# A three-pass graph network in fp32 halves: one stage's stores on another queue, uniform tail rows, a split first block and four empty steps

## The reference

```python
def _gc(x, adj, W, b):
    return adj @ (x @ W) + b
h = jnp.maximum(_layernorm(x, axis=-1), 0.0)
h = relu(_gc(h, adj, W1, b1))
h = relu(_gc(h, adj, W2, b2))
out = x + _gc(h, adj, W3, b3)
```

## Time and profile before

| | |
|---|---|
| median of 3 runs | 1595.33 us (1593.61 to 1596.07) |
| profiled execution | 1592.36 us, span of its instructions 1590.6 us |
| PE busy | 1580.9 us (99%) |
| PEld, DVE, ACT, POOL busy | 86%, 55%, 38%, 29% |
| DMA | 303 MB, mean 191 GB/s |

### The profile page before, as it was taken

One profiled execution on the slowest core, in us unless ns is written; L12 is line 12 of the kernel. 1 busy time (PEld: TensorE's weight loads), 2 busy tenths in 40 slices (PEclk: granted clock), 3 DMA queues, 4 the chain that ended last, 5 costly groups with the idle time before them and its releaser, 6 DMA issues.

```text
span 1590.6 us, 20924 instructions
## 1 busy us (share of the span) xinstructions
PE 1580.9 (99%) x7674; PEld 1360.6 (86%) x7674; DVE 874.1 (55%) x1358; ACT 608.8 (38%) x1073; POOL 464.4 (29%) x417
## 2 busy tenths in 40 slices
PE   9999999999999999999999999999999999999999
PEld 7888889988889898989898989788898887888898
DVE  8973433256544443434564446664565537766856
ACT  5542222233433332323332333443455435454444
POOL 5864544336655000000000015345402314301302
PEclk9999999999999999999999999999999999999999
DMA  7966657744567554545455658883644437887866
GB/s 246 333 211 209 220 188 213 201 137 148 182 210 230 167 153 143 142 119 149 142 170 160 179 184 288 274 301 125 206 136 117 100 86 213 247 247 220 250 192 192
DMA packets 196628, 303.37 MB, mean 191 GB/s; under 512 B 22632, under 2 KB 92608, under 8 KB 196524
## 3 DMA queue, kind: packets, MB, share of 16 engines
q1 hardware_dynamic: 162268, 223.12, 47.4%
q0 software_dynamic: 12224, 43.16, 8.3%
q10 hardware_dynamic: 22032, 35.74, 6.3%
HBM read 219.44 MB, written 82.50 MB: 190 GB/s over the span
## 4 chain that ended last, share of the span: by engine, by line
PE 96%; DVE 1%; DMA 1%; POOL 1%; ACT 0%; issue 0%; SPq 0%; DVEq 0%; ACTq 0%
PE ps L1707 32%; PE ps L1708 32%; PE ps L1709 32%; PE ps L1795 1%; DVE ring L1336 1%; DMA raw<-TS 1%; POOL stash L1550 0%; PE ps L1740 0%; DMA xin<-x 0%; DVE parts L1479 0%; POOL stash L1552 0%; ACT ring L1119 0%; DVE S L1383 0%; POOL stash L1554 0%; DVE stats L1267 0%
## 5 line engine op out<-in xcount | busy, mean ns | idle before, releaser
L1336 DVE TENSOR_TENSOR ring<-raw,ring 128x512 fp32r<-128x512 f32 (+1 forms) x562 | 405.7, 734 | 424.7 <-ACT ring L1119 422.0
L1119 ACT CAST ring<-raw 128x512 fp32r<-128x512 f32 (+1 forms) x562 | 320.7, 577 | 560.2 <-PE ps L1709 465.2
L1707 PE MATMUL ps<-slots,still 128*128 128x512 f32 (+1 forms) x504 | 184.1, 365 | 1.8 <-DVE still L1308 1.7
L1708 PE MATMUL ps<-slots,still 128*128 128x512 f32 (+1 forms) x504 | 183.7, 365 | 0.0
L1709 PE MATMUL ps<-slots,still 128*128 128x512 f32 (+1 forms) x504 | 183.7, 364 | 0.0
L1708 PE MATMUL ps<-ring,even 128*128 128x512 f32 (+1 forms) x480 | 174.4, 363 | 0.0
L1707 PE MATMUL ps<-ring,even 128*128 128x512 f32 (+1 forms) x480 | 174.4, 363 | 0.0
L1709 PE MATMUL ps<-ring,even 128*128 128x512 f32 (+1 forms) x480 | 174.4, 363 | 0.0
L1563 POOL DMA_DIRECT2D prep<-P x40 | 26.5, 664 | 462.0 <-DMA P<-U 430.1
L1707 PE MATMUL ps<-ring,S 128*128 128x512 f32 (+1 forms) x420 | 153.4, 365 | 2.1 <-DVE ring L1336 1.9
L1708 PE MATMUL ps<-ring,S 128*128 128x512 f32 (+1 forms) x420 | 152.9, 364 | 0.0
(11 more groups left out here) (160 smaller groups left out, 2902.6 us busy)
## 6 DMA issues: line engine op xcount, KB each, us to landing
raw<-TS SPq DMA_DIRECT2D x160, 256.0 KB, 2.9
raw<-adjT SPq DMA_DIRECT2D x138, 256.0 KB, 3.2
raw<-adjT SPq DMA_DIRECT2D x41, 512.0 KB, 4.6
TS<-made SPq DMA_DIRECT2D x20, 1024.0 KB, 6.7
raw<-TS SPq DMA_DIRECT2D x80, 165.0 KB, 2.4
raw<-HS SPq DMA_DIRECT2D x50, 256.0 KB, 2.7
raw<-P SPq DMA_DIRECT2D x45, 256.0 KB, 3.9
raw<-adjT SPq DMA_DIRECT2D x68, 165.0 KB, 2.6
```

What stands on the lines that cost most here:

```text
L1119: act.copy(hi, src).then_inc(hi_done, 1)
L1336: dve.tensor_tensor(lo, src, hi.bitcast(F32), ALU.subtract).then_inc(lo_done, 1)
L1707: pe.matmul(out, st_hi, mv_hi, start=start, stop=False)
L1708: pe.matmul(out, st_hi, mv_lo, start=False, stop=False)
```

## The change

Four edits. (1) Four empty steps are put into `late` between the combines of pairs 8 and 9 and their S2 stationaries. (2) REP becomes 128, so that all operands of the short block have 128 rows or columns. (3) For the very first x block ACT and DVE work in four pieces of 128 columns, and PE waits for the piece that the column group m needs. (4) POOL issues the store of `made` itself, right behind the four operations of a pair; SP no longer does.

```diff
@@ w3_phase
                     for pair, bufs in ((8, a), (9, z)):
                         late.append(lambda pair=pair, bufs=bufs: combine(pair, bufs))
                         late.append(lambda: None)
+                    late.extend([lambda: None] * 4)
@@ gcn_kernel
-    REP = 2 * STEP + TAIL
+    REP = P
@@ sync
-            def store_made(i):
-                t = ORDER[i % PAIRS]
-                c = i // PAIRS
-                sp.wait_ge(made_done, 4 * (i + 1))
-                sp.dma_start(TS[t, :, :, within(c)], made[:, i % 2, :, 0:WIDTH[c]]).then_inc(made_stored[i % 2], 16)
...
-                while j.pair_freed is not None and stores < j.pair_freed:
-                    store_made(stores)
-                    stores += 1
...
-            while stores < made_total:
-                store_made(stores)
-                stores += 1
@@ scalar, cut1
+                    if n == 0:
+                        for m in range(KF):
+                            cols = slice(m * P, (m + 1) * P)
+                            act.activation(still[:, j.block, 0, cols], tile[:, cols], ACT.Relu,
+                                           scale=x_column(n, "scale")) \
+                                .then_inc(first_hi if m < KF - 1 else hi1_done, 1)
+                        root(1)
+                        centre(1)
+                        return
@@ vector, cut1
+                if j.kind == "x" and j.q == 0:
+                    for m in range(KF):
+                        cols = slice(m * P, (m + 1) * P)
+                        if m < KF - 1:
+                            dve.wait_ge(first_hi, m + 1)
+                        else:
+                            dve.wait_ge(hi1_done, j.cut + 1)
+                        dve.scalar_tensor_tensor(still[:, j.block, 1, cols], xin[:, j.block, 1, cols],
+                                                 x_column(0, "scale"),
+                                                 still[:, j.block, 0, cols].bitcast(F32), ALU.mult, ALU.subtract) \
+                            .then_inc(first_lo if m < KF - 1 else lo1_done, 1)
+                    return
@@ gpsimd, make
+                pool.wait_ge(made_done, 4 * (i + 1))
+                pool.dma_start(TS[ORDER[n], :, :, within(c)], made[:, i % 2, :, 0:w]) \
+                    .then_inc(made_stored[i % 2], 16)
@@ tensor, pass 1
-                    pe.wait_ge(lo1_done, j.ready)
+                    pe.wait_ge(lo1_done, j.cut + 1 if j.a == 0 else j.ready)
...
+                        if j.a == 0 and a == 0:
+                            if m < KF - 1:
+                                pe.wait_ge(first_lo, m + 1)
+                            else:
+                                pe.wait_ge(lo1_done, j.ready)
```

More of the change, by code:

```diff
@@ L769, in gcn_kernel @@
         lo1_done = sem("lo1_done")
+        first_hi = sem("first_hi")
+        first_lo = sem("first_lo")
         slot1_used = sem("slot1_used")
@@ L884, in load_x @@
                 sp.dma_start(xin[:, b, 1, :], x[b * P:(b + 1) * P, :]).then_inc(x_in[b], 16)
-            def store_made(i):
-                t = ORDER[i % PAIRS]
-                c = i // PAIRS
-                sp.wait_ge(made_done, 4 * (i + 1))
-                sp.dma_start(TS[t, :, :, within(c)], made[:, i % 2, :, 0:WIDTH[c]]).then_inc(made_stored[i % 2], 16)
-            stores = 0
             load_x(xs1[0])
```

## The result

The changed kernel is slower: median 1601.72 us of 11 runs (1595.37 to 1610.08), against 1593.61 us of 11 runs of the kernel before (1592.22 to 1598.83). The ratio is 1.0049, 95% interval 1.0035 to 1.0064, about 8 us. The forecast was 1592.0 us with a range up to 1595.8. The profiled execution took 1601.72 us (span 1599.9), so it stands at the median; that of before took 1592.36.

A forecast was written before the change was run, and what follows sets the result against it. PE, busy 1580.9 of 1590.6 us, was taken as the bound, with DVE near-bound from 20 to 68 us. The terms -1.4 - 2.1 + 0.4 - 0.2 = -3.3 us gave a median of 1592.0 us, range 1588.8 to 1595.8.

The forecast's parts named there:

- Edit 4: Stores of `made` issued by POOL: DVE about 0.5 us less busy before 68 us; -0.2 us, bounds -0.3 and +1.7.
- upper bound of 1.7 us: POOL back to back in pass 1's start, nearly one pair more before 68 us, costing 1.85 us of DVE.
- Rival C: In DVE's full stretch, POOL's descriptor writing keeps DVE's two-input operations out: +8 or so, net +5, 1600 us; chance 0.05.
- POOL's own numbers: For stores of `made` from POOL: issue about 1.1 us, landing 7 us, 7.7 us per pair, no holding by the store.
- Edit 1: Empty steps before the S2 to S4 stationaries remove PE's wait near 1326 us: -1.4 us, bounds -1.4 and -0.4.
- Rival D: The wait near 1326 us only shifts, another cast standing behind POOL's chain: about -2.3 us in all, 1593.0; chance 0.09.
- Edit 2: 128 rows in tail matmuls of L1795 and L1740: 64 x 0.033 us saved, -2.1 us, bounds -2.6 and 0.
- Rival A: The tail matmuls' row count costs nothing, so 128 rows gain nothing: sum -1.2 us, 1594.1; chance 0.20.
- Rival B: Uniform rows also bring 330-column matmuls to 0.150 us: 1.7 us more in pass 1's last chunk, 1590.0; chance 0.14.
- Edit 3: First x block in four pieces: PE begins about 0.5 us earlier, DVE's chain grows; +0.4 us, bounds 0 and +0.5.

The follow-up runs named there:

- the break: The changed kernel with a one-element memset on POOL behind each store of `made` and a wait for it: 1589.58 us, ratio 0.9976 to the kernel before.
- the tiny transfer: The changed kernel with the stores of `made` back on SP and a 512-byte POOL transfer in their place: 1603.64 us, ratio 1.0061 to the kernel before.
- the waits between: The changed kernel with each POOL subtraction of a pair waiting for the one before it: 1593.62 us, ratio 1.0005 to the kernel before.
- the break without stores: The changed kernel with stores of `made` back on SP, POOL keeping a memset and its wait: 1595.15 us, ratio 1.0006 to the kernel before.

## Why the prediction was wrong

**Edit 4, the step that failed.** It was "So the 1.1 us of issue are free time for DVE", and from it -0.2 us. Measured: +9.5 us alone, and 9.2 us between the changed kernel and the one without edit 4 (1.0049 against 0.9991). The row it rested on, a DVE subtraction of 0.69 inside an issue of 0.73, was read rightly and shows too little: no POOL subtraction stood behind that issue. The issue does leave DVE free, as the 1.22 us with the break show. The price is paid behind it: at three places of chunk 0 the queued subtractions shut DVE out, for up to 4 us. The prediction itself gave DVE "about 2" us to spare there. Its own upper bound of 1.7 us came from POOL running back to back, but priced DVE's share as if POOL still gave way after each operation.

**Rival C** (slower, 1600, chance 0.05) named the place, the engine kept out and nearly the size, but its mechanism, descriptor writing that keeps DVE out, is not what happens: 512 bytes do the same as 1 MB, and a memset after the same issue cures it. Its chance was too small because one row was taken to settle what a DMA issue does among subtractions.

**POOL's own numbers.** The issue took 0.73 us, not 1.1, and the landing 6.5, not 7 (first the tile view of the changed kernel, min/median/max in ns, then the page's DMA issues):

```profile
L1532 POOL DMA_DIRECT2D TS<-made x30: 726/726/851, 25.0 to 307.8; - x30
```

```profile
TS<-made POOLq DMA_DIRECT2D x20, 1024.0 KB, 6.5
```

The seven pairs from 18.21 to 72.30 us follow one another every 7.0 to 8.2 us, 7.7 in the mean, as forecast. POOL waits 1.1 us in all for a store (0.95 and 0.17), where none was forecast. So POOL's own pace was right; what it does to DVE was not.

**Edit 1** did what was said: no wait of PE near 1326, and ACT's S2 cast of pair 9 waits 0.19 us for POOL instead of 3.06. Rival D (the wait only moves) is out: no wait of PE stands behind 1168 us. The size, -1.42, is just what the stretch from the W3 stage to the last chunk of pass 3 is shorter by with edit 1 alone; the ratios fit it but do not resolve it by themselves.

**Edit 2** gained what its row was read for and lost it again where the sum had put nothing. PE's timeline around pass 1's tails in the changed kernel, the first and the last of eight:

```profile
130.06 0.39 PE L1759 MATMUL ps<-slot_tail,still_tail 128*128 128x512 f32 x1
...
136.40 0.39 PE L1759 MATMUL ps<-slot_tail,still_tail 128*128 128x512 f32 x1
```

7 sets in 6.34 us are 0.906 each, where before had 0.934. Behind pass 1 it is uneven: pass 2's tails still go at 0.93 a set (549.47 to 552.26 for three), pass 3's matmuls at 0.227. Over the 512-column matmuls around all tails the starts lie 1.2 us closer in sum, forecast 2.1. Against that stand three 330-column stretches of pass 2, which went from 0.150 to 0.153 a matmul and cost 1.26 us. So edit 2 alone is worth about nothing, as its ratio of 0.9997 has it. Rival A (no gain) gave the right size for the wrong reason: the row count does change the spacing, in both directions. Why it does stays open.

Rival B (330-column matmuls at 0.150 throughout, 1.7 us more) came for its one chunk in the changed kernel: the last chunk of pass 1 took 76.80 us instead of 78.48. But of the ten profiled kernels with edit 2, four have it still at 0.153 there, edit 2 alone among them, so uniform rows alone do not bring it; and pass 2 went the other way.

**Edit 3** cost 0.36 us where +0.4 was forecast. PE began at 7.12 instead of 7.45, and its second half at 10.96 instead of 10.60:

```profile
10.96 0.50 PE L1721 MATMUL ps<-slots,still 128*128 128x512 f32 x1 [0.85 <-DVE slots L1337]
```

## What to carry to other kernels

A DMA issue put on GpSimd ahead of its own queued two-input operations can, though it need not, shut VectorE's two-input operations out for three of them in a row; look at what stands behind the issue, not at the issue. Where VectorE is the near-bound, a short operation and a wait for it behind the issue (0.24 us here) give it back, or the issues are put where VectorE has slack. A duration read where the neighbours are idle bounds nothing for a place where they are queued, and a rival's chance should not rest on one such row. A change of shape is to be looked for in all stages that use it: edit 2 gained beside one kind of matmul and lost as much beside another.

## What the runs showed of the hardware

- Behind a DMA issue on POOL, of 1 MB or of 512 bytes, POOL's next three subtractions can run 1.25 us apart, and a DVE operation begun during the issue then takes 5.40 or 5.19 us instead of 1.22. In the kernel before, without the issue, a POOL subtraction gave way (2.27 for the second), and no two-input DVE operation in chunk 0 took more than 2.20. What inside the engines keeps their order was not measured; only that a break of 0.24 us changes it.
- It does not happen at every store: in chunk 0 of the changed kernel it does at three (issues at 24.99, 47.90 and 71.62) and not at two others (32.15 and 39.69) where DVE came due just as far behind the start of the issue. What tells them apart was not found. Which executions have it where would explain the wide spread of the changed kernel's runs and of those with edit 4 alone (14 us in each), but the kernel with the tiny transfer spread only 2 us over its five runs, so the link is not shown.
- After PE's waits of 6.93, 6.16, 4.30, 4.19 and 2.70 us (the changed kernel, the tiny transfer, edit 4 alone, the waits between, the break without stores) some 6 to 14 matmuls started about 0.43 us apart, the 1.2 GHz level. Among waits near 2 us it went both ways: after 2.20 (edit 1 alone, at 1032 us) and 1.93 (the tiny transfer, at 32 us) eight did, after 2.15 and 2.14 (the changed kernel and edit 4 alone, at 32 us) none.
- The same 330-column matmuls start 0.150 us apart in some stages and kernels and 0.153 in others, at full granted clock and without a wait between them.
- Waits of 0.3 to 2.2 us between 1029 and 1168 us come and go between executions and were not pursued.
